# A mixture of experts whose scatters add into one table, with the combining spread over three engines

## The chip, the cores and the metric

One core of a Trainium2 chip runs the whole program. The metric is the device time of one execution in microseconds, as the median of several runs. The engines are TensorE (PE, with its weight loads as PEld), VectorE (DVE), ScalarE (ACT), GpSimd (POOL) and SyncE (SP). SP and POOL issue the data transfers (DMAs) that matter here: SP the plain ones, POOL the indirect ones, in which each of 128 partitions names its own row in memory.

## What is computed

The input is 8 sequences of 1024 tokens, 128 features each, in float32. A Mamba-style mixer and an MLP come first, and then the mixture of experts, in which the change lies. Cut to that part:

```python
x = x + _layernorm(_L0_attn_ref(_layernorm(x), ...))
x = x + _layernorm(_L0_ffn_ref(_layernorm(x), ...))

# _L0_ffn_ref, E = 8 experts, K = 2 of them for each token, N = 8192 tokens
probs = softmax(x @ Wr + br)
gates, ids = top_k(probs, K)
cap = ceil(1.2 * N / E)                       # the best gated tokens of an expert, by rank
xg = x[disp_tok].reshape(E, cap, 128)         # gather of the tokens of each expert
h = silu(einsum(xg, W1) + b1)
out = einsum(h, W2) + b2
gated = out * disp_g
y = zeros((N, 128)).at[disp_tok].add(gated)   # a token gets the sum of up to two experts
```

## The kernel before, in words

The program is a chain of stages with a barrier between two of them: a first stage (normalisation and decays, to about 60 us), the scan (to about 349 us), the MLP with the routing logits (to 513 us), the choice of the tokens of each expert (to 613 us), the experts (to 832 us) and the combining (to the end). Within a stage each engine runs its own instruction stream in a written order, and semaphores (`need`, `wait_ge`) make it wait for the others.

**MLP.** 32 groups of two token tiles run through a software pipeline, `skewed8`, that names for each engine its steps and by how many groups each lags. The last two steps on TensorE are `turn_xl` (L1380, lag 11), which transposes the normalised group into the PSUM bank `pX`, and `route` (L1387, lag 12), which makes the logits in `pL`. Between them ScalarE copies `pX` to `xlT` (L1253); VectorE takes the logits (L1330). TensorE's order within a step is `route` of group g-1, then `turn_xl` of group g, and `turn_xl` waits until ScalarE has copied the group before out of the single bank.

**Experts.** The slots of the eight experts are 80 columns of 128 rows, in 24 blocks of 2 to 4 columns, three blocks for each expert. POOL's stream is `fetch` of block i (one gather of 128 token rows for each column, L1871) and then `leave` of block i-5 (one scatter of 128 result rows for each column, L1879). `leave` waits for the block's result `yo`, which VectorE multiplies by the gates (L1992) from the PSUM bank `e_pB` that TensorE filled. A token has two rows in the table `choice_rows`: one for its first expert and one for its other, at a distance of 8192 rows, and `choice_of` holds the row to which a slot writes. No row is written twice. SP zeroes the table in the first stage with 16 transfers (L259), since a dropped token leaves a row unwritten, and POOL waits for that before its first gather. In the experts' stage SP loads the weights, and then waits for the scatters of the last eight blocks (L1851).

**Combining.** 64 token tiles are 14 groups of four tiles and five narrow ones of 2, 2, 2, 1 and 1. For each group SP loads both rows of the tokens (L1854, L1855), TensorE adds them in PSUM by two products with the identity (L1931), VectorE takes statistics of each tile (L2000) and joins them (L2006), ScalarE takes the root (L1959), VectorE inverts it (L2012) and forms the shift (L2014), ScalarE normalises each tile out of PSUM (L1965), VectorE adds the residual `x1` (L2019), and SP stores the group (L1859). VectorE's order in a step is: statistics of group g, inverse and shift of g-1, joining of g, residual of g-2. SP keeps eight groups of loads ahead of its stores. Ahead of this TensorE runs 18 products on zeros (L1925).

Of the kernel before, what the change touches and what calls it, by code (L numbers as in the profile page):

```python
# [32 lines left out]
P = 128  # L33
# [20 lines left out]
FILLS = 2 * TOKENS // (8 * P)  # L54
ROWLEN = D + 2
STEEP = 2.0 ** 100
# [21 lines left out]
def skewed(eng, steps, unroll, head, stages):  # L78


    def at(i, which):
# [12 lines left out]
    for i in range(steps, steps + max(lag for lag, _ in stages)):  # L94
        at(i, None)


def build(nc, x, ln_w, ln_b, in_proj_w, conv_w, conv_b, dt_bias, A_log, D_skip, rms_w, out_proj_w,
          mlp_w1, mlp_b1, mlp_w2, mlp_b2, Wr, br, W1, b1, W2, b2, out):
    table = nc.dram_tensor("token_rows", (TOKENS, ROWLEN), F32, kind="Internal").ap()  # L100
    choice = nc.dram_tensor("choice_rows", (2 * TOKENS, D), F32, kind="Internal").ap()
    decays = nc.dram_tensor("decay_rows", (2, P, TILES * HEADS), F32, kind="Internal").ap()
    with ExitStack() as ctx:
# [49 lines left out]
        token_of, choice_of = (sb(n, [P, COLS], U32) for n in ("token_of", "choice_of"))  # L153
# [23 lines left out]
        with ExitStack() as st:  # L177
# [58 lines left out]
            def _(sp):  # L236
# [19 lines left out]
                zeros = choice.rearrange("(n p r) d -> n p (r d)", p=P, r=8)  # L256
# [881 lines left out]
        with ExitStack() as st:  # L1138
# [23 lines left out]
            pT, pX, pM0, pM1, pL = (pst("m_" + n) for n in ("pT", "pX", "pM0", "pM1", "pL"))  # L1162
# [16 lines left out]
            def skewed8(eng, stages):  # L1179

                skewed(eng, GROUPS, 8, 16, stages)
# [33 lines left out]
            def _(a):  # L1215
# [34 lines left out]
                def turned_xl(g, m):  # L1250
                    need(a, s_px, g)
                    need(a, s_pl, g, NB)
                    a.activation(xlT[:, m % NB, :], pX[:, 0:N], ACT.Copy).then_inc(s_xlT, 1)  # L1253
# [92 lines left out]
            def _(pe):  # L1346
# [42 lines left out]
                skewed8(pe, [(5, down), (3, up), (12, route), (2, turn), (11, turn_xl)])  # L1389


        with ExitStack() as st:
# [186 lines left out]
            def _(v):  # L1579
# [156 lines left out]
                link(v.scalar_tensor_tensor(out=acc[:, 1, :], in0=is_other[:, :], scalar=float(TOKENS - TILES), in1=vacant[:, :],  # L1736
                                            op0=ALU.mult, op1=ALU.add))
                link(v.tensor_copy(choice_of[:, :], acc[:, 1, :]))
# [6 lines left out]
        with ExitStack() as st:  # L1745
# [16 lines left out]
            def pst(name, shape=[P, 512]):  # L1762
# [12 lines left out]
            widths = [CG] * 14 + [2, 2, 2, 1, 1]  # L1775
# [4 lines left out]
            yb = arena2[:, 0:TILES * D].rearrange("p (t d) -> p t d", d=D)  # L1780
# [6 lines left out]
            (s_ys2, s_st, s_var, s_sd, s_rs, s_sh, s_yna, s_ot, s_out) = (  # L1787
                sem("c_" + n) for n in ("ys", "st", "var", "sd", "rs", "shift", "yna", "ot", "out"))
            first_v = choice[0:TOKENS].rearrange("(p s b) d -> s p b d", s=STEPS, p=P)
            other_v = choice[TOKENS:2 * TOKENS].rearrange("(p s b) d -> s p b d", s=STEPS, p=P)  # L1790
            out_v = out.rearrange("b (s p) d -> s p b d", p=P)

            def of_group(g):
                return slice(first_tile[g], first_tile[g + 1])

# [13 lines left out]
            banks = pT + pH + [pO, pB]  # L1809
            BANKS = len(banks)  # L1810

            def summed(g):
                return banks[g % BANKS][:, 0:D * widths[g]]
# [27 lines left out]
            def _(sp):  # L1841
# [11 lines left out]
                def load(g):  # L1853
                    sp.dma_start(ys[:, of_group(g)], part(first_v, g)).then_inc(s_in[g], 16)  # L1854
                    sp.dma_start(yb[:, of_group(g)], part(other_v, g)).then_inc(s_in[g], 16)  # L1855

                def store(g):
                    need(sp, s_ot, g)
                    sp.dma_start(part(out_v, g), ys[:, of_group(g)]).then_inc(s_out, 16)  # L1859
# [4 lines left out]
            def _(g):  # L1864
# [10 lines left out]
                def leave(n):  # L1875
                    need(g, s_yo, n)
                    for i in range(sizes[n]):
                        c = starts[n] + i
                        g.indirect_dma_start(choice, bass.IndirectOffsetOnAxis(ap=choice_of[:, c:c + 1], axis=0),  # L1879
                                             yo[:, n % RING, i, :], None, bounds_check=2 * TOKENS - 1,  # L1880
                                             oob_is_err=False).then_inc(s_scat[n % RING], 16)
                g.wait_ge(filled, 16 * FILLS)
                staged([(0, fetch), (LAG, leave)])

            @block.tensor
            def _(pe):
# [40 lines left out]
                def both(g):  # L1927
                    pe.wait_ge(s_in[g], 32)
                    need(pe, s_yna, g, BANKS)
                    for f, first in ((ys, True), (yb, False)):  # L1930
                        ins = pe.matmul(summed(g), ident[:, :], f[:, of_group(g)].rearrange("p t d -> p (t d)"), start=first, stop=not first)  # L1931
                    ins.then_inc(s_ys2, 1)
                in_turn(GROUPS, [(0, both)])

            @block.scalar
            def _(a):
# [33 lines left out]
            def _(v):  # L1970
# [25 lines left out]
                def moments(g):  # L1996
                    need(v, s_var, g, 2)
                    need(v, s_ys2, g)
                    for i in range(widths[g]):
                        ins = v.bn_stats(c_st[:, g % 2, i, :], summed(g)[:, D * i:D * (i + 1)])  # L2000
# [16 lines left out]
                def add_x1(g):  # L2017
# [27 lines left out]
```

## Time and profile before

| what | us |
|---|---|
| median of 3 runs | 878.65 (876.77 to 880.98) |
| the profiled execution, whole time | 879.82 |
| its span, first to last instruction | 878.1 |
| experts' stage, first gather to first load of the combining | 613.64 to 832.75 |
| combining, first load to the end of the span | 832.75 to 878.1 |

The profile is of one execution, with times from the start of its span. A row of the timeline is: start in us, duration in us, engine, line of the program, operation, what it writes and reads, how many instructions the row merges, and in brackets how long the engine had been idle and what ended that. "issue" means that the engine waited for nothing that the profile shows. Shapes are partitions x elements. The whole time is 1.72 us more than the span, and the profiled execution is 1.17 us above the median.

### The profile page before, as it was taken

The numbers are of one execution on the slowest core, as the hardware profiler recorded it, in microseconds if no ns is written. First come the engines' busy times: TensorE is split into PE (matmuls) and PEld (weight loads), VectorE is DVE, ScalarE is ACT, GpSimd is POOL, SyncE is SP. The second block draws the span as 40 slices with busy tenths as digits, with TensorE's granted clock in tenths as the row PEclk, the third lists the DMA queues.
The fourth block names the chain that finished last, engine by engine and source line by source line (L and its number), as shares of the span: only waits on it lengthen the run. The fifth ranks groups of instructions, "written<-read, shape, count | busy, mean of one in ns | idle before, by whom it ended". The sixth has DMA issues, their size and how long they took to land. (4 is left out here: it accounts for less than half of the span.)

```text
span 878.1 us, 14619 instructions
## 1 busy us (share of the span) xinstructions
PE 710.7 (81%) x3872; PEld 493.1 (56%) x3872; DVE 606.9 (69%) x2161; ACT 490.8 (56%) x1207; POOL 442.8 (50%) x576
## 2 busy tenths in 40 slices
PE   7657999999999997899999721046698888888994
PEld 3425677777777775798989720023354444444442
DVE  7957999999999993799999868897111211121067
ACT  4864666676667675687877415434243432334157
POOL 7612767667667664234433350000757777777500
PEclk8867999999999999999999855555699998999998
DMA  9930000000000001500000004000322212221196
GB/s 219 388 129 14 1 1 1 2 1 1 2 1 1 1 1 34 159 1 2 3 1 1 1 0 196 0 0 2 99 64 72 74 50 74 73 75 50 41 352 219
DMA packets 50414, 52.92 MB, mean 60 GB/s; under 512 B 7576, under 2 KB 39624, under 8 KB 50080
## 3 DMA queue, kind: packets, MB, share of 16 engines
q1 hardware_dynamic: 44496, 41.62, 14.6%
q0 software_dynamic: 5120, 10.37, 4.4%
q8 instruction: 30, 0.49, 0.2%
q14 instruction: 48, 0.39, 0.1%
q10 hardware_dynamic: 720, 0.05, 0.1%
HBM read 28.04 MB, written 24.18 MB: 59 GB/s over the span
## 5 line engine op out<-in xcount | busy, mean ns | idle before, releaser
L890 DVE SCALAR_TENSOR_TENSOR s_cv<-s_pU,tap_w,s_cv 128x256 f32<-128x256 f32 x372 | 153.4, 476 | 12.4 <-ACT s_cv L821 12.0
L1871 POOL DMA_INDIRECT arena<-token_rows,token_of x80 | 81.4, 1017 | 112.3 <-issue 111.7
L1992 DVE TENSOR_TENSOR arena<-e_pB,e_gate 128x384 f32<-128x384 f32 (+2 forms) x24 | 14.5, 603 | 123.9 <-PE e_pB L1916 123.9
L1879 POOL DMA_INDIRECT choice_rows<-arena,choice_of x80 | 79.7, 996 | 32.7 <-issue 22.6
L1943 ACT ACTIVATE e_h<-e_pH,e_bcols 128x384 f32<-128x384 f32 (+2 forms) x96 | 58.7, 616 | 65.6 <-PE e_pH L1900 63.1
L1900 PE MATMUL e_pH<-e_xgT,e_w 128*128 128x384 f32 (+2 forms) x192 | 83.4, 584 | 0.0
L689 POOL TENSOR_TENSOR s_xa<-s_xt,arena 128x512 f32<-128x512 f32 x32 | 34.5, 1077 | 88.3 <-ACT s_xt L839 88.3
L821 ACT ACTIVATE s_cv<-s_pU,tap_b,tap_w 128x256 f32<-128x256 f32 x124 | 63.7, 561 | 23.4 <-PE s_pU L723 23.0
L723 PE MATMUL s_pU<-arena,w_in 128*128 128x262 f32 x248 | 69.3, 403 | 7.7 <-DVE s_cv L890 3.4
L1908 PE MATMUL e_pO<-e_h,e_w 128*128 128x384 f32 (+2 forms) x192 | 72.7, 522 | 0.4 <-ACT e_oT L1950 0.4
L1372 PE MATMUL m_pM<-w_m,m_h 128*128 128x128 f32 x512 | 62.5, 275 | 0.1
L1363 PE MATMUL m_pH<-m_hT,w_m 128*128 128x256 f32 x256 | 60.7, 380 | 2.1 <-ACT m_h L1246 1.5
L1372 PEld LDWEIGHTS m_pM<-w_m,m_h 128*128 128x128 f32 x512 | 59.7, 192 | 0.3 <-issue 0.3
L1900 PEld LDWEIGHTS e_pH<-e_xgT,e_w 128*128 128x128 f32 x192 | 40.1, 220 | 28.9 <-issue 21.2
L1908 PEld LDWEIGHTS e_pO<-e_h,e_w 128*128 128x128 f32 x192 | 36.7, 191 | 33.3 <-issue 20.6
L1207 POOL TENSOR_TENSOR arena<-arena,m_un 128x256 f32<-128x256 f32 (+1 forms) x32 | 22.5, 703 | 64.9 <-DVE m_un L1282 64.9
L723 PEld LDWEIGHTS s_pU<-arena,w_in 128*128 128x128 f32 x248 | 43.0, 197 | 17.0 <-DVE s_cv L890 7.6
L1363 PEld LDWEIGHTS m_pH<-m_hT,w_m 128*128 128x128 f32 x256 | 46.2, 190 | 7.5 <-ACT m_hT L1239 2.6
L1246 ACT ACTIVATE m_h<-m_pH,b_col 128x256 f32<-128x256 f32 x128 | 50.2, 485 | 0.0
L1984 DVE COPY e_xgT<-e_pT 128x384 f32<-128x384 f32 (+2 forms) x24 | 14.4, 599 | 48.3 <-PE e_pT L1891 48.3
L1950 ACT ACTIVATE e_oT<-e_pO,e_bcols 128x384 f32<-128x384 f32 (+2 forms) x24 | 14.8, 617 | 54.8 <-PE e_pO L1908 54.8
L701 POOL TENSOR_TENSOR s_y<-s_y,s_dx 128x512 f32<-128x512 f32 x32 | 40.9, 1277 | 4.9 <-DVE s_y L923 4.9
(305 smaller groups left out, 1874.3 us busy)
## 6 DMA issues: line engine op xcount, KB each, us to landing
choice_rows<-zrow SPq DMA_DIRECT2D x16, 512.0 KB, 7.7
arena<-choice_rows SPq DMA_DIRECT2D x28, 256.0 KB, 5.3
token_rows<-arena SPq DMA_DIRECT2D x8, 520.0 KB, 5.8
n_x<-in_L_attn_x_dram SPq DMA_DIRECT2D x8, 512.0 KB, 7.6
arena<-in_L_attn_x_dram SPq DMA_DIRECT2D x8, 512.0 KB, 4.8
e_w<-in_L_ffn_W_dram SPq DMA_DIRECT2D x16, 256.0 KB, 3.2
out_dram<-arena SPq DMA_DIRECT2D x14, 256.0 KB, 4.2
decay_rows<-arena SPq DMA_DIRECT2D x2, 1024.0 KB, 4.8
```

Source lines behind the costliest of these rows:

```text
L701: g.tensor_tensor(y2[:, :], y1[:, p % 2, :], dx[:, p % 4, :], ALU.add).then_inc(s_y2, 1)
L723: pe.matmul(pU[m % 2][:, 0:G2 * XBLK], w_in[:, P * m:P * (m + 1)], xT[:, G2 * p:G2 * (p + 1), :].rearrange("p t c -> p (t c)"), start=True ...
L821: a.activation(by_tile(cv[:, p % 2, m, :]), columns(m)[:, :, 0:P], ACT.Identity, bias=tap_b[:, m:m + 1], scale=tap_w[:, m, 0:1]).then_inc( ...
L890: v.scalar_tensor_tensor(out=by_tile(cv[:, p % 2, m, :]), in0=columns(m)[:, :, tap:tap + P], scalar=tap_w[:, m, tap:tap + 1], in1=by_tile( ...
L1246: ins = a.activation(h1[:, m % NB, c, :], pH[half_][:, N * (c % 2):N * (c % 2 + 1)], ACT.Relu, bias=b1_col[:, c:c + 1])
L1363: ins = pe.matmul(pH[half_][:, N * c:N * (c + 1)], w_m1[:, P * f:P * (f + 1)], hT[:, m % NB, :], start=True, stop=True)
L1372: ins = pe.matmul(pM[m % 2][:, P * i:P * (i + 1)], h1[:, m % NB, c, P * i:P * (i + 1)], w_m2[:, c, :], start=(c == 0), stop=(c == NF - 1))
L1871: g.indirect_dma_start(xg[:, n % RING, i, :], None, table, bass.IndirectOffsetOnAxis(ap=token_of[:, c:c + 1], axis=0), bounds_check=TOKENS ...
L1879: g.indirect_dma_start(choice, bass.IndirectOffsetOnAxis(ap=choice_of[:, c:c + 1], axis=0), yo[:, n % RING, i, :], None, bounds_check=2 * ...
L1900: pe.matmul(pH[c][:, 0:w], we1[:, expert(n) % 2, P * c:P * (c + 1)], xgT[:, n % 3, 0:w], start=True, stop=True).then_inc(s_ph, 1)
L1908: ins = pe.matmul(pO[:, 0:w], we2[:, expert(n) % 2, c, :], hb[:, n % 2, c, 0:w], start=(c == 0), stop=(c == NF - 1))
L1943: a.activation(hb[:, n % 2, c, 0:w], pH[c][:, 0:w], ACT.Silu, bias=bcols[:, f:f + 1]).then_inc(s_h, 1)
```

## The change

Five things are changed.

1. The table `choice_rows` of 16384 rows becomes `summed_rows` of 8192, one row for each token; both experts of a token scatter into the same row, and the scatter adds to what is there (`compute_op=ALU.add`). `target_of` takes the place of `choice_of`. SP zeroes it with 8 transfers.
2. A token's two experts are never the same, so no two scatters of one expert meet in a row, but those of two experts can. Ahead of an expert's first block POOL therefore waits until all scatters of the expert before have landed.
3. In the combining SP loads one row for each token, and TensorE has no part in it; statistics and normalisation read SBUF. In the 14 wide groups ScalarE normalises three tiles, VectorE the fourth (`normal_last`), and GpSimd adds the residual (`add_x1_wide`). In the five narrow groups ScalarE normalises and VectorE adds, as before. The 18 products on zeros are gone.
4. In the MLP `pX` becomes two banks, and in the last steps, when no new group enters, TensorE runs `turn_xl` of group g ahead of `route` of group g-1 (`at_end`).
5. The threshold `STEEP`, from which a slower way through the scan is chosen, goes from 2^100 to 2^62.

The core of the diff:

```diff
-FILLS = 2 * TOKENS // (8 * P)
+FILLS = TOKENS // (8 * P)
-STEEP = 2.0 ** 100
+STEEP = 2.0 ** 62
...
     for i in range(steps, steps + max(lag for lag, _ in stages)):
-        at(i, None)
+        at(i, None, at_end or stages)
...
-                for n in range(2 * TOKENS // (8 * P)):
+                for n in range(FILLS):
                     sp.dma_start(zeros[n], zrow[:, :]).then_inc(filled, 16)
...
+            pX = [pst("m_pX0"), pst("m_pX1")]
...
-                    need(pe, s_xlT, g, 1)
+                    need(pe, s_xlT, g, 2)
                     for i in range(G):
-                        ins = pe.transpose(pX[:, P * i:P * (i + 1)], xl[:, m % NB, i, :], ident[:, :])
+                        ins = pe.transpose(pX[m % 2][:, P * i:P * (i + 1)], xl[:, m % NB, i, :], ident[:, :])
...
-                skewed8(pe, [(5, down), (3, up), (12, route), (2, turn), (11, turn_xl)])
+                skewed8(pe, [(5, down), (3, up), (12, route), (2, turn), (11, turn_xl)],
+                        at_end=[(5, down), (3, up), (11, turn_xl), (12, route), (2, turn)])
...
                 def load(g):
-                    sp.dma_start(ys[:, of_group(g)], part(first_v, g)).then_inc(s_in[g], 16)
-                    sp.dma_start(yb[:, of_group(g)], part(other_v, g)).then_inc(s_in[g], 16)
+                    sp.dma_start(ys[:, of_group(g)], part(summed_v, g)).then_inc(s_in[g], 16)
...
                 def leave(n):
                     need(g, s_yo, n)
+                    if expert(n) and n % STEP == 0:
+                        for m in range(n - STEP, n):
+                            g.wait_ge(s_scat[m % RING], 16 * blocks_upto(m))
                     for i in range(sizes[n]):
                         c = starts[n] + i
-                        g.indirect_dma_start(choice, bass.IndirectOffsetOnAxis(ap=choice_of[:, c:c + 1], axis=0),
-                                             yo[:, n % RING, i, :], None, bounds_check=2 * TOKENS - 1,
-                                             oob_is_err=False).then_inc(s_scat[n % RING], 16)
+                        g.indirect_dma_start(summed, bass.IndirectOffsetOnAxis(ap=target_of[:, c:c + 1], axis=0),
+                                             yo[:, n % RING, i, :], None, bounds_check=TOKENS - 1, oob_is_err=False,
+                                             compute_op=ALU.add).then_inc(s_scat[n % RING], 16)
...
+                def add_x1_wide(g_):
+                    need(g, s_yna, g_)
+                    need(g, s_ynv, g_)
+                    g.tensor_tensor(yn[:, of_group(g_)], yn[:, of_group(g_)], x1[:, of_group(g_), :], ALU.add).then_inc(s_otp, 1)
+                in_turn(WIDE_GROUPS, [(0, add_x1_wide)])
...
-                need(pe, s_xgT, TOTAL - 1)
-                for _ in range(18):
-                    pe.matmul(pT[0][:, :], ones[:, :], zrow[:, 0:512], start=True, stop=True)
...
-                    for i in range(widths[g]):
+                    for i in range(on_act(g)):
                         t = first_tile[g] + i
-                        ins = a.activation(ys[:, t, :], summed(g)[:, D * i:D * (i + 1)], ACT.Identity, bias=c_sh[:, g, i:i + 1], scale=c_rs[:, g, i:i + 1])
+                        ins = a.activation(yn[:, t, :], ys[:, t, :], ACT.Identity, bias=c_sh[:, g, i:i + 1], scale=c_rs[:, g, i:i + 1])
...
-                        ins = v.bn_stats(c_st[:, g % 2, i, :], summed(g)[:, D * i:D * (i + 1)])
+                        ins = v.bn_stats(c_st[:, g % 2, i, :], ys[:, first_tile[g] + i, :])
...
+                def normal_last(g):
+                    if g < WIDE_GROUPS:
+                        t = first_tile[g] + CG - 1
+                        need(v, s_rs, g)
+                        v.tensor_scalar(yn[:, t, :], ys[:, t, :], c_mv[:, g, CG - 1, 0:1], c_rs[:, g, CG - 1:CG],
+                                        ALU.subtract, ALU.mult).then_inc(s_ynv, 1)
...
-                in_turn(GROUPS, [(0, moments), (1, inverse), (0, combined), (2, add_x1)])
+                in_turn(GROUPS, [(0, moments), (1, inverse), (0, combined), (1, normal_last), (2, add_x1_narrow)])
```

On POOL, near the end of the experts' stage, before: the last two gathers (of block 23) stand between the scatters of blocks 17 and 18; then only scatters follow. `e_yo` is VectorE's result; the names at the gathers are the semaphores that say a ring buffer is free.

```order
L1879 DMA choice_rows<-arena,choice_of 16384x128 x2
L1871 DMA arena<-token_rows,token_of 128x130 [waits s_row,n_shifted,s_mr]
L1871 DMA arena<-token_rows,token_of 128x130
L1879 DMA choice_rows<-arena,choice_of 16384x128 [waits e_yo]
L1879 DMA choice_rows<-arena,choice_of 16384x128 x3
```

The same place now; block 18 is the first of expert 6. `n_post`, `n_pre` and `n_convs` are earlier names of the semaphores that count the scatters of blocks 15 to 17.

```order
L1884 DMA summed_rows<-arena,target_of 8192x128 x2
L1873 DMA arena<-token_rows,token_of 128x130 [waits s_xfirst,s_row,s_mm]
L1873 DMA arena<-token_rows,token_of 128x130
L1884 DMA summed_rows<-arena,target_of 8192x128 [waits n_post,n_pre,n_convs,e_yo]
L1884 DMA summed_rows<-arena,target_of 8192x128 x3
```

The order of gathers and scatters is the same; seven scatters (the first of experts 1 to 7) now also wait for three blocks' landings. Ahead of that of expert 7, block 21, stand no gathers, only the scatters of blocks 19 and 20. The fourteen residual adds stand behind the last scatter on this engine.

On VectorE, one step of the combining in its steady part, before:

```order
L2000 BN_STATS c_stats<-e_pH 128x6 x4
L2012 RECIPROCAL c_rs<-c_sd 128x4
L2014 SCALAR_TENSOR_TENSOR c_shift<-c_mv,c_rs 128x4
L2006 BN_AGGR c_mv<-c_stats 128x2 x4
L2019 TENSOR_TENSOR arena<-arena 128x512
```

and now:

```order
L1999 BN_STATS c_stats<-arena 128x6 x4
L2011 RECIPROCAL c_rs<-c_sd 128x4
L2013 SCALAR_TENSOR_TENSOR c_shift<-c_mv,c_rs 128x4
L2005 BN_AGGR c_mv<-c_stats 128x2 x4
L2020 TENSOR_SCALAR arena<-arena,c_mv,c_rs 128x128
```

The statistics read SBUF (`arena`) in place of PSUM, and the residual add over four tiles has become the normalisation of one.

## Rows read from the trace of the kernel before

**Rows 1.** Windows: us; PE, PEld, DVE, ACT, POOL busy (count); PEclk; DMA share; GB/s.

```profile
613.00:832.00 219.00, 183.12 (x570) 101.46 (x571) 35.63 (x120) 76.25 (x123) 161.02 (x160) 0.91 0.25 67
832.00:878.10 46.10, 33.80 (x88) 15.62 (x86) 32.48 (x185) 27.83 (x83) 0.00 (x0) 0.92 0.83 275
```

**Rows 2.** The page's costliest groups: the gathers and the scatters.

```profile
L1871 POOL DMA_INDIRECT arena<-token_rows,token_of x80 | 81.4, 1017 | 112.3 <-issue 111.7
L1879 POOL DMA_INDIRECT choice_rows<-arena,choice_of x80 | 79.7, 996 | 32.7 <-issue 22.6
```

**Rows 3.** Timeline of POOL and SP, experts' stage to the combining's first load.

```profile
613.64 1.26 POOL L1871 DMA_INDIRECT arena<-token_rows,token_of  x1 [88.18 <-issue]
...
798.56 0.98 POOL L1879 DMA_INDIRECT choice_rows<-arena,choice_of  x1 [0.30 <-issue]
...
802.52 1.02 POOL L1879 DMA_INDIRECT choice_rows<-arena,choice_of  x1 [0.30 <-issue]
...
815.74 0.98 POOL L1879 DMA_INDIRECT choice_rows<-arena,choice_of  x1 [0.30 <-issue]
818.90 0.98 POOL L1879 DMA_INDIRECT choice_rows<-arena,choice_of  x1 [2.18 <-DVE arena L1992]
...
830.49 0.98 POOL L1879 DMA_INDIRECT choice_rows<-arena,choice_of  x1 [0.30 <-issue]
832.75 0.33 SPq L1854 DMA_DIRECT2D arena<-choice_rows  x1
```

**Rows 4.** DMA issues: what, queue, count, KB each, us from issue to landing.

```profile
arena<-token_rows,token_of POOLq DMA_INDIRECT x80, 2.6
choice_rows<-arena,choice_of POOLq DMA_INDIRECT x80, 2.3
e_w<-in_L_ffn_W_dram SPq DMA_DIRECT2D x16, 256.0 KB, 3.2
```

**Rows 5.** Timeline of VectorE in the combining: first, one steady step, last.

```profile
838.73 0.89 DVE L2000 BATCH_NORM_STATS2 c_stats<-e_pT 128x6 f32<-128x128 f32 x4 [16.75 <-PE e_pT L1931]
...
845.46 0.88 DVE L2000 BATCH_NORM_STATS2 c_stats<-e_pH 128x6 f32<-128x128 f32 x4
846.46 0.16 DVE L2014 SCALAR_TENSOR_TENSOR c_shift<-c_mv,c_rs 128x4 f32<-128x4 f32 x1
846.83 0.66 DVE L2019 TENSOR_TENSOR arena<-arena 128x512 f32<-128x512 f32 x1
847.40 0.88 DVE L2000 BATCH_NORM_STATS2 c_stats<-e_pH 128x6 f32<-128x128 f32 x4
...
874.43 0.29 DVE L2019 TENSOR_TENSOR arena<-arena 128x128 f32<-128x128 f32 x1 [0.24 <-ACT arena L1965]
```

**Rows 6.** Timeline, first stage: VectorE's shift beside a GpSimd operation.

```profile
22.66 1.47 POOL L307 TENSOR_TENSOR n_hn<-n_hc,n_scale 128x768 f32<-128x768 f32 x1
23.08 1.08 DVE L525 SCALAR_TENSOR_TENSOR n_shift<-moments,n_scale 128x8 f32<-128x8 f32 x1
```

**Rows 7.** All of line L525: count, ns min/median/max, first and last start.

```profile
L525 DVE SCALAR_TENSOR_TENSOR n_shift<-moments,n_scale x8: 1076/1080/1372, 10.2 to 32.0; 128x8 f32<-128x8 f32 x8
```

**Rows 8.** Timeline, end of the MLP: normalisations on VectorE beside a GpSimd add.

```profile
486.39 0.59 DVE L1282 TENSOR_SCALAR m_un<-m_at,m_mv,m_rs 128x128 f32<-128x128 f32 x2
486.88 0.97 DVE L1282 TENSOR_SCALAR m_xl<-arena,m_mv,m_rs 128x128 f32<-128x128 f32 x2
487.05 0.72 POOL L1207 TENSOR_TENSOR arena<-arena,m_un 128x256 f32<-128x256 f32 x1 [1.84 <-DVE m_un L1282]
```

**Rows 9.** A page group: GpSimd's add of 128x512 in the scan.

```profile
L701 POOL TENSOR_TENSOR s_y<-s_y,s_dx 128x512 f32<-128x512 f32 x32 | 40.9, 1277 | 4.9 <-DVE s_y L923 4.9
```

**Rows 10.** Timeline of TensorE in the last groups of the MLP.

```profile
508.00 1.02 PE L1387 MATMUL m_pL<-w_r,m_xlT 128*128 128x8 f32 x4 [0.47 <-ACT m_xlT L1253]
508.88 0.67 PE L1380 MATMUL m_pX<-ident,m_xl 128*128 128x128 f32 x2
510.02 1.02 PE L1387 MATMUL m_pL<-w_r,m_xlT 128*128 128x8 f32 x4 [0.47 <-ACT m_xlT L1253]
```

More of the change, by code:

```diff
@@ L75, in need_apart, with skewed, at @@
         eng.sem_inc(carrier[0], 1)
-def skewed(eng, steps, unroll, head, stages):
-    def at(i, which):
+def skewed(eng, steps, unroll, head, stages, at_end=None):
+    def at(i, which, stages=stages):
         for lag, stage in stages:
@@ L151, in build @@
         ssq = sb("ssq", [P, TILES])
-        token_of, choice_of = (sb(n, [P, COLS], U32) for n in ("token_of", "choice_of"))
+        token_of, target_of = (sb(n, [P, COLS], U32) for n in ("token_of", "target_of"))
         is_other, is_first = (sb(n, [P, COLS]) for n in ("is_other", "is_first"))
@@ L1161, in build @@
             xlT = sbt("m_xlT", [P, NB, N])
-            pT, pX, pM0, pM1, pL = (pst("m_" + n) for n in ("pT", "pX", "pM0", "pM1", "pL"))
+            pT, pM0, pM1, pL = (pst("m_" + n) for n in ("pT", "pM0", "pM1", "pL"))
+            pX = [pst("m_pX0"), pst("m_pX1")]
             pM = [pM0, pM1]
@@ L1177, in build, with skewed8 @@
             block = st.enter_context(nc.Block())
-            def skewed8(eng, stages):
-                skewed(eng, GROUPS, 8, 16, stages)
+            def skewed8(eng, stages, at_end=None):
+                skewed(eng, GROUPS, 8, 16, stages, at_end)
             @block.sync
@@ L1735, in _ @@
                 link(v.tensor_tensor(vacant[:, :], vals[:, :], vacant[:, :], ALU.add))
[L1736 removed]
+                link(v.scalar_tensor_tensor(out=acc[:, 1, :], in0=is_other[:, :], scalar=-float(TILES), in1=vacant[:, :],
                                             op0=ALU.mult, op1=ALU.add))
[L1738 removed]
+                link(v.tensor_copy(target_of[:, :], acc[:, 1, :]))
                 link(v.scalar_tensor_tensor(out=vals[:, :], in0=is_other[:, :], scalar=-float(TILES), in1=vals[:, :],
@@ L1786, in build @@
             s_in = [sem(f"c_in{g}") for g in range(GROUPS)]
[L1787 to L1790, printed above, removed]
+            (s_st, s_var, s_sd, s_rs, s_sh, s_yna, s_ynv, s_otp, s_otv, s_out) = (
+                sem("c_" + n) for n in ("st", "var", "sd", "rs", "shift", "yna", "ynv", "otp", "otv", "out"))
+            summed_v = summed.rearrange("(p s b) d -> s p b d", s=STEPS, p=P)
             out_v = out.rearrange("b (s p) d -> s p b d", p=P)
@@ L1794, in of_group, with on_act @@
                 return slice(first_tile[g], first_tile[g + 1])
+            def on_act(g):
+                return CG - 1 if g < WIDE_GROUPS else widths[g]
             def part(v_, g):
@@ L1853, in load @@
                 def load(g):
-                    sp.dma_start(ys[:, of_group(g)], part(first_v, g)).then_inc(s_in[g], 16)
-                    sp.dma_start(yb[:, of_group(g)], part(other_v, g)).then_inc(s_in[g], 16)
+                    sp.dma_start(ys[:, of_group(g)], part(summed_v, g)).then_inc(s_in[g], 16)
                 def store(g):
-                    need(sp, s_ot, g)
-                    sp.dma_start(part(out_v, g), ys[:, of_group(g)]).then_inc(s_out, 16)
+                    if g < WIDE_GROUPS:
+                        need(sp, s_otp, g)
+                    else:
+                        need(sp, s_otv, g - WIDE_GROUPS)
+                    sp.dma_start(part(out_v, g), yn[:, of_group(g)]).then_inc(s_out, 16)
                 in_turn(GROUPS, [(0, load), (8, store)])
@@ L1921, in _ @@
                 staged([(2, up), (3, down), (4, back), (0, turn)])
-                need(pe, s_xgT, TOTAL - 1)
-                for _ in range(18):
-                    pe.matmul(pT[0][:, :], ones[:, :], zrow[:, 0:512], start=True, stop=True)
[L1927 to L1933, printed above, removed]
             @block.scalar
@@ L1997, in moments @@
                     need(v, s_var, g, 2)
-                    need(v, s_ys2, g)
+                    v.wait_ge(s_in[g], 16)
                     for i in range(widths[g]):
-                        ins = v.bn_stats(c_st[:, g % 2, i, :], summed(g)[:, D * i:D * (i + 1)])
+                        ins = v.bn_stats(c_st[:, g % 2, i, :], ys[:, first_tile[g] + i, :])
                     ins.then_inc(s_st, 1)
```

23 lines of the change are left out of this document (11 added, 12 removed).

## The prediction, made before the changed kernel ran

> **What bounds the kernel now.** I read the windows of the two changed stages first, then the costliest groups, then the timeline of POOL in the one and of VectorE in the other.
>
> In the experts' stage POOL is the bound. From the first gather at 613.64 to the last scatter at 830.49 it issues 160 indirect DMAs [rows 3]; a gather takes 1.017 us and a scatter 0.996 [rows 2], with 0.30 us behind each, and three steps of the stream, from the scatter at 798.56 to that at 802.52, take 3.96 us, so 1.32 each [rows 3]. 160 of these are 211 us of the 217 between those rows. TensorE is busy for 183 of the stage's 219 us [rows 1], but POOL issues a block's gathers five blocks ahead of its scatters, so what TensorE does is late only at the end, where the POOL rows show waits for VectorE's results (2.18 us before 818.90).
>
> In the combining VectorE is the bound. Its step for a wide group is 1.94 us (statistics at 845.46, the next at 847.40) and has no gap: 1.00 to the shift at 846.46, 0.37 to the residual add at 846.83, 0.57 to the next statistics [rows 5]. It starts late, 5.98 us after the first load (832.75 to 838.73), since a group needs two loads and TensorE's sum first [rows 3, 5].
>
> In the last groups of the MLP nothing is busy throughout. One group follows another at 2.02 us (508.00 to 510.02) on a ring: route, then the transposition 0.88 later, then 1.14 until ScalarE's copy lets the next route start [rows 10].
>
> **Edit 4, the MLP's end.** With two banks the transposition of group g runs ahead of the route of g-1, and the copy runs beside that route. What is left on TensorE is 0.88 for the route and 0.67 for the transposition [rows 10], 1.55 a group in place of 2.02. Four groups at the end go at this pace, so 4 x 0.47 = -1.9 us. The bounds are 0 (if VectorE's inputs are late instead) and six groups, -2.8. In the loop the order is unchanged and its wait was met by the route before it, so nothing moves there.
>
> **Edits 1 and 5, the tables and the threshold.** The eight zero-fills that go stand on SP's queue behind the loads that the first stage waits for, and POOL asks for them only before 613.64: nothing. The threshold matters only if the inputs cross it; from the reference's own inputs the largest exponent of the decays within half a chunk is about 2^35, under both thresholds, so the same way is taken.
>
> **Edit 1, the scatter that adds.** Their count and place on POOL stay. No row shows an adding scatter. The nearest rows are gather and scatter, which move rows in opposite directions and differ by 0.02 us [rows 2]: I take no extra time on POOL. The bound from above is an adding scatter as dear as one gather and one scatter together, since it reads the row and writes it: 80 x 1.02 = +82 us. A gain has no reason, as nothing is left out of the instruction.
>
> The Trainium skill (DMA: Bandwidth & Descriptors, "Anatomy of one DMA") says that generating descriptors is a small part of a DMA from GpSimd, and that many can be emitted before it shows. By it the extra time is near zero, as taken; no row here varies the number.
>
> Landing is the second cost. A plain scatter lands 2.3 us after its issue, a gather 2.6 [rows 4]. An adding one lies between 2.3 and a gather and a scatter in turn, 4.9; I take +1.0, nearer to the plain one, because the row in memory can be read while the row in SBUF is.
>
> **Edit 2, the waits.** Ahead of the first block of an expert, POOL now waits for the last scatter of the expert before. Between the two stand the gathers of a later block. At expert 6 there are two: the scatter at 798.56, the next at 802.52, so 3.96 us of cover against a landing of 3.3 [rows 3, 4]. Experts 1 to 5 have three or four gathers, 5.3 us or more. Both cover it, and cost nothing; without that cover each would cost a landing. Behind the waiting scatter on POOL stand the gathers for later blocks, five blocks ahead of need. At expert 7 no gather is left: the scatter at 818.90 follows that at 815.74 and already waits there for VectorE [rows 3], so of the landing the extra 1.0 is exposed. The same 1.0 is exposed behind the last scatter (830.49), for which SP waits before the first load (832.75). Together +2.0 us, between 0 and 5.2.
>
> **Edit 3, the combining.** It starts earlier: one load of 256 KB, which lands in 3.2 us where little else runs [rows 4], and no sum on TensorE. VectorE starts 3.3 us after the first load in place of 5.98.
>
> VectorE's own step becomes 1.00 + 0.37 as now, and 0.25 for one tile's normalisation (two stand at 486.39 and the next at 486.88 [rows 8]) where the add took 0.57: 1.62 us. ScalarE has three tiles in place of four. But GpSimd now adds 128x512 for each group, and that took 1.277 us [rows 9]. The rows show what VectorE does beside such an operation. A shift of 128x8 takes 1.08 us, all eight of them [rows 6, 7], and ends when GpSimd's does (22.66 + 1.47 = 24.13; 23.08 + 1.08 = 24.16); the same operation over 128x4 takes 0.16 where GpSimd is idle [rows 5]. Two tiles normalised take 0.59 us alone and 0.97 beside GpSimd's add [rows 8]. These are the very two operations, shift and normalisation, that stand in VectorE's new step. So shift, joining and normalisation (0.08 + 0.29 + 0.25 = 0.62 us) and the 1.277 of GpSimd exclude each other but for the joining. At best GpSimd starts behind the normalisation, and a step is 1.28 + 0.62 + 0.1 for two hand-overs = 2.0 us. At worst it starts between shift and normalisation, and a step is 1.62 + 1.28 less the joining, 2.6. I take 2.3, the middle, since GpSimd's start hangs on ScalarE and falls in either place. That is more than the 1.94 of now.
>
> The sum from the first load: 3.3 to start, 1.2 and 1.6 for two steps before GpSimd has work, 12 x 2.3 = 27.6, together 33.7. The narrow groups took from 866.8 (845.46 + 11 x 1.94) to the end of VectorE at 874.72 (874.43 + 0.29), 7.9 us [rows 5]; two wide adds of 0.57 leave this stretch and one normalisation enters, 7.0. Together 40.7 against 42.0 now (832.75 to 874.72): -1.3 us. With 2.0 a step it is -4.9, with 2.6 +2.3. The store behind is the same, and the loads, half as many, run ahead.
>
> **The sum.** -1.9 (MLP) + 2.0 (landings) - 1.3 (combining) = -1.2. On the profiled 879.82 that is 878.6; this execution lies 1.17 above the median, so the forecast for the median is 877.5 us. A measurement of this kernel can tell about 0.5%, 4.4 us, from no change.
>
> **Rivals.** *VectorE is not held up.* If GpSimd's adds fall so that VectorE's two operations miss them, or the exclusion doesn't hold here, the step is 1.62: 3.3 + 1.2 + 1.6 + 12 x 1.62 + 7.0 = 32.5, 9.5 us less than now, and the kernel takes 869. For it speaks that only two short operations of each step are at risk; against it the eight of eight shifts [rows 7].
>
> *POOL pays for the adding.* If the adding makes POOL write three ends of a transfer for a row (source, old value, result) where a plain one has two, and its time goes by what it writes, each scatter takes half of 0.996 more [rows 2]: 80 x 0.5 = +40, so 917. It decides from 0.07 us a scatter on, which makes 80 x 0.07 = 5.6 against the -1.2. For it speaks that POOL has no slack in this stage [rows 1 to 3]; against it that POOL's two kinds cost the same.
>
> The Trainium skill (Collectives: The Full Stack, "Why ReduceScatter is half of AllGather") says that a transfer that reduces emits two reading descriptors for each chunk where a copy emits one. No row here shows whether POOL's time follows it; by it this rival's 917 would be the time.
>
> *The landings are not covered.* If an adding scatter lands after 8 us, five boundaries stall for 2.7 and one for 4.0, and expert 7 and the end each show 5.7: 29 us, so 904 with the other terms. It decides from a landing of 5.5 us on. Against it speak 2.3 and 2.6 [rows 4].
>
> **How the numbers follow.** The forecast has 0.40, with its own range of 871 to 882: MLP 0 to -2.8, landings 0 to 5.2, steps of 2.0 to 2.6. Of it 0.10 falls below 874 (steps near 2.0), 0.28 within 0.5%, 0.02 above. VectorE not held up has 0.30, POOL's price 0.22, uncovered landings 0.08. So faster 0.40, same 0.28, slower 0.32. The range goes from 867, under the first rival with a little more at the MLP's end, to 900, which takes in an extra 0.28 us a scatter; what is left out is the upper part of the other two rivals, some 0.15, and little below.
>
> **What would show it.** Right: scatters of 1.0 us with 1.3 from start to start; POOL's first scatters of experts 1 to 6 without a wait, that of expert 7 about 1 us later; shift and normalisation in the wide groups often near 1 us in place of 0.16 and 0.33, a step of about 2.3 us; last logits about 2 us sooner. Wrong: scatters longer than 1.07 us; waits at the boundaries; a VectorE step of 1.6.

## The result: the adding is paid on POOL

The changed kernel takes 919.6 us (median of 4 runs, 919.4 to 920.68) against 878.36 for the kernel before (876.77 to 880.98): a ratio of 1.0467, 95% interval 1.0451 to 1.0483. It is slower by 41 us, outside the range given. The profiled execution took 919.78, with a span of 917.7.

The costliest groups of the changed kernel (line, engine, operation, count; busy us and mean ns of one; idle time ahead of it), its software queue that carries gathers and scatters (packets, MB, share), and the scatter's landing:

```profile
L1873 POOL DMA_INDIRECT arena<-token_rows,token_of x80 | 82.5, 1031 | 112.3 <-issue 110.2
L1884 POOL DMA_INDIRECT summed_rows<-arena,target_of x80 | 126.2, 1578 | 29.7 <-issue 23.2
...
q0 software_dynamic: 14080, 10.37, 8.6%
...
summed_rows<-arena,target_of POOLq DMA_INDIRECT x80, 3.3
```

Against [rows 2] the gather has kept its price and the scatter has gone from 996 to 1578 ns. In the kernel before the same queue line reads:

```profile
q0 software_dynamic: 5120, 10.37, 4.4%
```

The bytes are the same and the packets are not. 5120 packets over 160 transfers are 32 each; 14080 less 80 gathers of 32 leave 144 for a scatter, 128 rows and 16 more. Landing is 3.3 us where it was 2.3 [rows 4].

POOL and SP at the places of [rows 3], in the timeline of the changed kernel (start, duration, engine, line; in brackets the idle time and what ended it):

```profile
610.83 1.26 POOL L1873 DMA_INDIRECT arena<-token_rows,token_of  x1 [88.22 <-issue]
...
849.12 1.55 POOL L1884 DMA_INDIRECT summed_rows<-arena,target_of  x1 [0.30 <-issue]
850.98 1.55 POOL L1884 DMA_INDIRECT summed_rows<-arena,target_of  x1 [0.30 <-issue]
854.96 1.55 POOL L1884 DMA_INDIRECT summed_rows<-arena,target_of  x1 [2.42 <-DMA summed_rows<-arena,target_of]
...
871.72 1.56 POOL L1884 DMA_INDIRECT summed_rows<-arena,target_of  x1 [0.31 <-issue]
874.90 4.23 SPq L1854 DMA_DIRECT2D arena<-summed_rows  x9
```

From start to start a scatter now takes 1.86 us (849.12 to 850.98); the 0.30 between two is as before. The stage from first gather to last scatter is 260.89 us, where it was 216.85. The only place where POOL waits for the landing of earlier scatters is the row at 854.96, the first scatter of expert 7. Its windows, columns as in [rows 1], for the experts and the combining:

```profile
610.00:874.00 264.00, 182.07 (x545) 101.01 (x545) 35.94 (x120) 76.12 (x123) 208.66 (x160) 0.84 0.35 56
874.00:917.70 43.70, 0.00 (x0) 0.00 (x0) 34.91 (x185) 24.75 (x69) 18.13 (x14) 0.50 0.64 193
```

POOL's busy time in the experts' stage goes from 161.02 to 208.66 with the same 160 instructions; TensorE's stays at 182, so it is further from the bound than before.

Where the spans differ, stretch by stretch, in us:

| stretch | before | after | difference |
|---|---|---|---|
| to the first gather | 613.64 | 610.83 | -2.8 |
| first gather to last scatter | 216.85 | 260.89 | +44.0 |
| last scatter to first load | 2.26 | 3.18 | +0.9 |
| first load to first statistics | 5.98 | 2.52 | -3.5 |
| first statistics to VectorE's end | 35.99 | 36.15 | +0.2 |
| VectorE's end to the end of the span | 3.38 | 4.13 | +0.8 |
| sum | 878.10 | 917.70 | +39.6 |

### The profile page after: what moved, and what is told of

Same layout as the page of the kernel before. It is cut to its first block and busy times, and to the rows that moved or that the text cites. A ratio compares the mean times of both kernels' runs of the same rounds, so it can differ in the third digit from the quotient of the medians.

```text
span 917.7 us, 14384 instructions
## 1 busy us (share of the span) xinstructions
PE 672.7 (73%) x3760; PEld 475.2 (52%) x3760; DVE 609.7 (66%) x2161; ACT 487.5 (53%) x1193; POOL 508.6 (55%) x590
## 3 DMA queue, kind: packets, MB, share of 16 engines
q0 software_dynamic: 14080, 10.37, 8.6%
## 5 line engine op out<-in xcount | busy, mean ns | idle before, releaser
L1884 POOL DMA_INDIRECT summed_rows<-arena,target_of x80 | 126.2, 1578 | 29.7 <-issue 23.2
L1911 PE MATMUL e_pH<-e_xgT,e_w 128*128 128x384 f32 (+2 forms) x192 | 91.5, 631 | 0.0
L1911 PEld LDWEIGHTS e_pH<-e_xgT,e_w 128*128 128x128 f32 x192 | 44.3, 243 | 33.6 <-issue 29.1
L1902 PE MATMUL e_pT<-ident,arena 128*128 128x128 f32 x80 | 17.3, 342 | 58.0 <-DMA arena<-token_rows,token_of 58.0
L1204 POOL TENSOR_TENSOR m_h0b<-m_h,b2row 128x256 f32<-128x256 f32 x32 | 23.3, 730 | 38.1 <-DVE m_h L1303 38.1
```

The lines of the kernel that those rows point to most:

```text
L1884: g.indirect_dma_start(summed, bass.IndirectOffsetOnAxis(ap=target_of[:, c:c + 1], axis=0), yo[:, n % RING, i, :], None, bounds_check=TOKE ...
L1911: pe.matmul(pH[c][:, 0:w], we1[:, expert(n) % 2, P * c:P * (c + 1)], xgT[:, n % 3, 0:w], start=True, stop=True).then_inc(s_ph, 1)
```

## The experiments

**The adding taken away.** If the adding alone costs, the changed kernel without it must fall back under the kernel before; if the shared table or the waits cost, it must not.

```diff
-                                             yo[:, n % RING, i, :], None, bounds_check=TOKENS - 1, oob_is_err=False,
-                                             compute_op=ALU.add).then_inc(s_scat[n % RING], 16)
+                                             yo[:, n % RING, i, :], None, bounds_check=TOKENS - 1, oob_is_err=False).then_inc(s_scat[n % RING], 16)
```

> The changed kernel with one thing undone: its scatters overwrite in place of adding (the addition in the scatter is left out, so a token's row holds one expert's result alone). One table, waits between experts, the new combining and the MLP's end stay. Theory: the adding alone makes a scatter dearer on POOL (1.58 us in place of 1.00), and nothing else lengthens the experts' stage. Then scatters take 1.00 us, 1.30 from start to start, the stage takes 217 us in place of 260.9, the landing falls from 3.3 to 2.3 us, and the whole time is 919.6 - 44 - 1 = about 874.5, under the kernel before. Rival: the one table of half the rows, or the waits between experts, make the scatters slow (rows in one table written by neighbouring experts, a queue that is drained seven times). Then scatters stay near 1.6 us and the time near 919.

It takes 875.95 us, 0.9973 of the kernel before (0.9956 to 0.9991). The scatter's group, and the first scatter of expert 7 in the timeline:

```profile
L1884 POOL DMA_INDIRECT summed_rows<-arena,target_of x80 | 79.6, 995 | 31.0 <-issue 22.9
...
813.81 0.98 POOL L1884 DMA_INDIRECT summed_rows<-arena,target_of  x1 [2.18 <-DVE arena L1990]
```

The scatter is back at 995 ns with one table and all seven waits in place, and the stage is 214.83 us. Of the 2.0 us by which this is under the kernel before, 1.6 are a shorter wait for VectorE ahead of the first scatter (3.52 us in place of 5.16), which the kernel with the MLP's end alone has too (3.50), with its scatters as they were. The wait for expert 6's landings is met while POOL waits for VectorE as before. So with plain scatters neither the shared table nor the waits cost anything; the adding does.

**The adding alone, in the kernel before.**

```diff
-                                             oob_is_err=False).then_inc(s_scat[n % RING], 16)
+                                             oob_is_err=False, compute_op=ALU.add).then_inc(s_scat[n % RING], 16)
```

> The kernel before with one thing added: its scatters add to the zeroed two-row table, where no row is written twice. No waits between experts, no other combining, no change in the MLP. Theory (the adding is the price): scatters take 1.57 us, 1.86 from start to start, 80 x 0.57 = 45.6 us more, of which the 2 us that POOL waited for VectorE near the end come back, and 0.9 more for the last landing: 878.4 + 45.6 - 2 + 0.9 = 923. Rival (waits or the shared table are the price): scatters stay at 1.0 us, and the time within 3 us of 878.

It takes 924.23 us, a ratio of 1.0523 (1.0492 to 1.0554). Its scatters, their landing, and the first scatter of expert 7:

```profile
L1879 POOL DMA_INDIRECT choice_rows<-arena,choice_of x80 | 126.2, 1578 | 27.7 <-issue 22.9
...
choice_rows<-arena,choice_of POOLq DMA_INDIRECT x80, 3.3
...
859.00 1.55 POOL L1879 DMA_INDIRECT choice_rows<-arena,choice_of  x1 [0.30 <-DVE arena L1992]
```

The price is the changed kernel's to the nanosecond, with no row written twice and no wait. With a slower POOL, VectorE is no longer late at 859.00 (2.18 us before). The stage is 258.79 us, 2.1 less than the changed kernel's 260.89: the 2.42 of the one exposed landing less the 0.30 that stands behind every scatter.

**What the price hangs on.** Two kernels with a different shape of scatter for each expert, one adding, one not:

```diff
+            SHAPES = [(P, D), (96, D), (64, D), (32, D), (16, D), (P, D // 2), (P, D // 4), (P, D)]
...
+                        r, w = SHAPES[expert(n)]
+                        to = summed if w == D else summed.rearrange("t (h d) -> (t h) d", d=w)
+                        g.indirect_dma_start(to, bass.IndirectOffsetOnAxis(ap=target_of[0:r, c:c + 1], axis=0),
+                                             yo[0:r, n % RING, i, 0:w], None, bounds_check=TOKENS - 1,
```

> The changed kernel with a different shape of scatter for each expert, all of them adding: expert 0 128 rows of 512 B, expert 1 96 rows, expert 2 64, expert 3 32, expert 4 16 rows of 512 B, expert 5 128 rows of 256 B, expert 6 128 rows of 128 B, expert 7 128 rows of 512 B (the remaining rows and columns of the results are left out, and the short rows go to other places of the table). To be read against the same shapes without the adding. Theory (POOL writes more for each row): the extra goes with the rows and not with the bytes: 0.58 us for 128 rows, 0.43 for 96, 0.29 for 64, 0.14 for 32, 0.07 for 16, and 0.58 again for 256 B and 128 B, in 128 + 16 packets a scatter. Rival 1 (a fixed cost of the adding kind): 0.58 in all of them. Rival 2 (bytes, or an adding transfer that moves slower and holds POOL back): 0.29 for 64 rows and for 256 B, 0.15 for 32 rows and for 128 B; the first scatters, which find an empty queue, would be shorter than the rest.

> The same eight shapes without the adding (it is left out, with the rows and columns named for the adding one). It gives the plain price for each shape. Theory: 1.00 us for 128 rows whatever their bytes, and less for fewer rows if POOL's time has a part for each row; if the plain time were all for rows, 0.5 for 64. Rival (a fixed cost): 1.00 for all rows.

The two kernels take 911.80 and 872.55 us, one run each; what is read is the single scatters. The last scatter of expert 0 (128 rows of 512 B), 2 (64 rows), 4 (16 rows) and 6 (128 rows of 128 B) in the timeline, and the queue's packets; first adding, then plain:

```profile
667.42 1.55 POOL L1888 DMA_INDIRECT summed_rows<-arena,target_of  x1 [0.30 <-issue]
729.18 1.41 POOL L1888 DMA_INDIRECT summed_rows<-arena,target_of  x1 [0.30 <-issue]
788.65 1.29 POOL L1888 DMA_INDIRECT summed_rows<-arena,target_of  x1 [0.30 <-issue]
843.38 1.55 POOL L1888 DMA_INDIRECT summed_rows<-arena,target_of  x1 [0.30 <-issue]
...
q0 software_dynamic: 11040, 8.12, 7.3%
```

```profile
663.82 0.98 POOL L1888 DMA_INDIRECT summed_rows<-arena,target_of  x1 [0.30 <-issue]
714.79 0.90 POOL L1888 DMA_INDIRECT summed_rows<-arena,target_of  x1 [0.30 <-issue]
764.71 0.84 POOL L1888 DMA_INDIRECT summed_rows<-arena,target_of  x1 [0.30 <-issue]
810.69 0.98 POOL L1888 DMA_INDIRECT summed_rows<-arena,target_of  x1 [0.30 <-issue]
...
q0 software_dynamic: 5120, 8.12, 3.9%
```

The last scatter of each expert, in us:

| shape | adding | plain | extra |
|---|---|---|---|
| 128 rows of 512 B | 1.55 | 0.98 | 0.57 |
| 96 rows | 1.42 | 0.92 | 0.50 |
| 64 rows | 1.41 | 0.90 | 0.51 |
| 32 rows | 1.32 | 0.86 | 0.46 |
| 16 rows | 1.29 | 0.84 | 0.45 |
| 128 rows of 256 B | 1.55 | 0.98 | 0.57 |
| 128 rows of 128 B | 1.55 | 0.98 | 0.57 |

The theory falls: with an eighth of the rows the extra is still 0.45 us where 0.07 was expected. The rival with the bytes falls too: rows of 128 B cost what rows of 512 B cost, and the first adding scatter, with no other in the queue, takes 1.63 us (at 641.00) and is no shorter than the rest. Most of the extra, some 0.44 us by these rows, is there for any adding scatter, and only about 0.12 goes with the rows from 16 to 128, about 1 ns a row. It is nearest to the rival of a fixed cost; what POOL does in that fixed time no run here shows. The packets do follow the rows: ten scatters of each shape with rows + 16 packets (four times 144, then 112, 80, 48 and 32) and 80 gathers of 32 make the 11040; plain ones have 32 in every shape. So the packets are no measure of POOL's time: 144 packets in place of 32, for 128 rows in place of 16, came with 0.12 us more of the extra.

**The MLP's end alone.** The kernel before with edit 4 (`pX` in two banks, `at_end`) and nothing else.

```diff
-                skewed8(pe, [(5, down), (3, up), (12, route), (2, turn), (11, turn_xl)])
+                skewed8(pe, [(5, down), (3, up), (12, route), (2, turn), (11, turn_xl)],
+                        at_end=[(5, down), (3, up), (11, turn_xl), (12, route), (2, turn)])
```

> The kernel before with the change to the MLP's end alone: two banks for the transposition, and in the last steps the transposition ahead of the route. Theory: a group at the end takes 1.35 us in place of 2.02, as the trace of the changed kernel shows, in four steps or a little more, so the last logits come 1.8 to 2.8 us sooner and the whole time is 875.6 to 876.6. The changed kernel's MLP also began 1.05 us sooner than that of the kernel before; if this comes of the eight zero-fills that are gone, it isn't here, and the MLP begins near 349.4; if it is a difference from one execution to the next, it may be anywhere between 348.3 and 349.4. Rival: the MLP's gain is lost again behind it, since the choice of the tokens waits for something else; then the time stays at 878.4.

It takes 875.79 us, 0.9971 of the kernel before (0.9955 to 0.9986): shorter by 0.3%, clear of the noise but far under 2%, and the least time here of a version that computes everything. TensorE in the last groups, where [rows 10] showed 2.02 us a group:

```profile
505.92 0.69 PE L1381 MATMUL m_pX<-ident,m_xl 128*128 128x128 f32 x2
506.40 0.87 PE L1388 MATMUL m_pL<-w_r,m_xlT 128*128 128x8 f32 x4
507.13 0.67 PE L1381 MATMUL m_pX<-ident,m_xl 128*128 128x128 f32 x2
507.64 0.99 PE L1388 MATMUL m_pL<-w_r,m_xlT 128*128 128x8 f32 x4
508.49 0.67 PE L1381 MATMUL m_pX<-ident,m_xl 128*128 128x128 f32 x2
508.99 0.99 PE L1388 MATMUL m_pL<-w_r,m_xlT 128*128 128x8 f32 x4
510.34 0.99 PE L1388 MATMUL m_pL<-w_r,m_xlT 128*128 128x8 f32 x4 [0.36 <-DVE logits L1331]
```

A route follows the last at 1.24 to 1.35 us, without a gap on TensorE until the last. In the changed kernel the MLP also begins 1.05 us sooner than in the kernel before (348.31 against 349.36), and so it does here. The first row of the MLP on VectorE tells that the zero-fills and the threshold are not the cause, since this kernel has all sixteen fills and the old threshold. First this kernel, then the kernel before:

```profile
348.22 0.61 DVE L1303 SCALAR_TENSOR_TENSOR m_h<-arena,m_rooty,m_res 128x128 f32<-128x128 f32 x2
```

```profile
349.36 0.35 DVE L1302 SCALAR_TENSOR_TENSOR m_h<-arena,m_rooty,m_res 128x128 f32<-128x128 f32 x1
```

In the kernel with the adding alone, which lacks edit 4 too, it stands at 349.50. Nor does edit 4 bring the lead by itself: the kernel with the plain shapes has it and begins the MLP at 349.36, and over all nine profiles this row lies between 347.67 and 349.50. The lead's cause stays open. Little of it lasts in the changed kernel: at the fifth route from the end it leads by only 0.08 us (503.93 against 504.01).

**The combining's split, undone in two ways.** In the changed kernel, first ScalarE takes all tiles and VectorE all residual adds again; then GpSimd's add is left out and nothing put in its place.

```diff
             def on_act(g):
-                return CG - 1 if g < WIDE_GROUPS else widths[g]
+                return widths[g]
...
-                in_turn(WIDE_GROUPS, [(0, add_x1_wide)])
...
-                in_turn(GROUPS, [(0, moments), (1, inverse), (0, combined), (1, normal_last), (2, add_x1_narrow)])
+                in_turn(GROUPS, [(0, moments), (1, inverse), (0, combined), (2, add_x1_narrow)])
```

> The changed kernel with the combining's split undone alone: ScalarE normalises all tiles and VectorE adds the residual in all groups, as in the kernel before, and GpSimd has no part. One load for a group and statistics from SBUF stay. Theory (GpSimd's add and VectorE's short operations exclude each other, which made a step 2.12 us): without GpSimd a step is VectorE's 1.00 + 0.37 + 0.57 = 1.94 us or a little less, the shift stays near 0.16 us, and with 14 groups the time is 2 to 3 us less than the changed kernel's, 917. Rival (the step of 2.12 is ScalarE's or the loads'): the step stays at 2.1 or grows, since ScalarE has four tiles again, and the time is 919.6 or above.

```diff
-                        need(sp, s_otp, g)
+                        need(sp, s_yna, g)
+                        need(sp, s_ynv, g)
...
-                in_turn(WIDE_GROUPS, [(0, add_x1_wide)])
```

> The changed kernel with GpSimd's residual add left out (the wide groups lack the residual), so that VectorE's step stands alone with three tiles on ScalarE and one on VectorE. Theory (exclusion): shift back to 0.16 us, a tile's normalisation to 0.3 us in all groups, a step of 1.62 us, so 14 x 0.5 = 7 us less than the changed kernel in the combining, about 912. Rival (the step was the loads' or ScalarE's): the step stays near 2.1.

What these are to be compared with is the combining of the changed kernel, VectorE and POOL in one view of the timeline each, over three groups:

```profile
881.78 0.87 DVE L1999 BATCH_NORM_STATS2 c_stats<-arena 128x6 f32<-128x128 f32 x4
...
883.23 1.32 DVE L2020 TENSOR_SCALAR arena<-arena,c_mv,c_rs 128x128 f32<-128x128 f32 x1
884.47 0.86 DVE L1999 BATCH_NORM_STATS2 c_stats<-arena 128x6 f32<-128x128 f32 x4
...
885.44 0.70 DVE L2013 SCALAR_TENSOR_TENSOR c_shift<-c_mv,c_rs 128x4 f32<-128x4 f32 x1
...
886.36 0.31 DVE L2020 TENSOR_SCALAR arena<-arena,c_mv,c_rs 128x128 f32<-128x128 f32 x1
...
887.93 0.31 DVE L2020 TENSOR_SCALAR arena<-arena,c_mv,c_rs 128x128 f32<-128x128 f32 x1
888.16 0.86 DVE L1999 BATCH_NORM_STATS2 c_stats<-arena 128x6 f32<-128x128 f32 x4
```

```profile
883.21 1.26 POOL L1893 TENSOR_TENSOR arena<-arena 128x512 f32<-128x512 f32 x1 [0.21 <-ACT arena L1964]
884.87 1.26 POOL L1893 TENSOR_TENSOR arena<-arena 128x512 f32<-128x512 f32 x1 [0.40 <-ACT arena L1964]
888.00 1.37 POOL L1893 TENSOR_TENSOR arena<-arena 128x512 f32<-128x512 f32 x1 [1.87 <-ACT arena L1964]
```

GpSimd adds from 883.21 to 884.47. VectorE's normalisation, issued at 883.23, ends at 884.55 and takes 1.32 us; the shift at 885.44 ends at 886.14, with GpSimd's next add (884.87 + 1.26 = 886.13). With GpSimd idle the normalisation at 886.36 takes 0.31, and so does that at 887.93, which starts just ahead of GpSimd's third add; there the add is the longer one, 1.37 in place of 1.26. The statistics keep their 0.86 in either case. Three groups take 888.16 - 881.78 = 6.38 us, 2.13 each.

With GpSimd's add left out, one step reads:

```profile
886.60 0.86 DVE L1999 BATCH_NORM_STATS2 c_stats<-arena 128x6 f32<-128x128 f32 x4
...
887.57 0.16 DVE L2013 SCALAR_TENSOR_TENSOR c_shift<-c_mv,c_rs 128x4 f32<-128x4 f32 x1
...
887.94 0.31 DVE L2020 TENSOR_SCALAR arena<-arena,c_mv,c_rs 128x128 f32<-128x128 f32 x1
888.17 0.86 DVE L1999 BATCH_NORM_STATS2 c_stats<-arena 128x6 f32<-128x128 f32 x4
```

The step is 1.57 us, all 14 normalisations lie between 310 and 319 ns and all 19 shifts between 158 and 164, and the kernel takes 911.04 (one run). From the first load to VectorE's end it is 31.71 us (874.80 to 906.51) in place of 38.67 in the changed kernel (874.90 to 913.57). So GpSimd's add costs VectorE 7 us here, and the loads and ScalarE allow the shorter step.

With the adds on VectorE two steps take 3.93 us (the statistics at 885.63 and 889.56), 1.97 each, and the shifts are back at 0.16. First load to VectorE's end is 37.78 us (873.83 to 911.61), 0.9 less than with GpSimd: less than the 2 to 3 expected. Early in the stretch VectorE waits 0.55 for ScalarE, which normalises four tiles again. The whole time, 919.89 (916.59 to 921.08), can't be told from the changed kernel's 919.6. So the split over three engines brings nothing over the split over two.

## Why the prediction was wrong

**Edit 1, extra time on POOL: the step that failed.** I took the adding scatter's time from the gather and the plain scatter, because they agreed, and set the extra to nothing. Both rows are of transfers that only copy; that they agree says that the direction doesn't matter, and nothing on a third kind of work. The bounds for an operation that no row showed were 0 and 1.02 us a scatter, with nothing to place it near either; the middle, 0.5, would have given 917, and my range stopped at 0.28. The scatters measured 0.58 more, 126.2 - 79.7 = 46.5 us, on an engine with no slack in this stage, which [rows 1 to 3] had shown rightly. The stage's +44.0 is 45.9 of these, for the 79 scatters that lie between its two ends, plus 1.1 for gathers 14 ns longer, less 3.0 for POOL's other waits. Those waits are, first before and then after:

```profile
644.84 1.03 POOL L1879 DMA_INDIRECT choice_rows<-arena,choice_of  x1 [5.16 <-DVE arena L1992]
...
813.17 0.98 POOL L1879 DMA_INDIRECT choice_rows<-arena,choice_of  x1 [1.90 <-DVE arena L1992]
```

```profile
640.36 1.64 POOL L1884 DMA_INDIRECT summed_rows<-arena,target_of  x1 [3.47 <-DVE arena L1991]
```

The first is 1.7 shorter, the second falls from 1.90 to the usual 0.30, and at expert 7 a landing of 2.42 stands where VectorE took 2.18. The first is not the slower POOL's doing, since the kernel without the adding has 3.52 there; against that kernel the stage is longer by 46.1 (260.89 against 214.83). The prediction let POOL wait for VectorE only at the end of the stage; the row at 644.84 shows that it waits at its start as well.

**The rival "POOL pays for the adding"** gave 917 and came within 3 us. Its mechanism was only part right, so that the closeness is in part luck. It let the time go by what POOL writes for a row, half of 0.996; the size, 0.58, is near, but the shapes show that it is mostly no matter of rows. The Trainium skill (Collectives: The Full Stack, "Why ReduceScatter is half of AllGather") gives two reading descriptors for a chunk that is reduced where a copy has one; the sum it led to was right in size, and the runs here can't show the descriptors themselves. The Trainium skill (DMA: Bandwidth & Descriptors, "Anatomy of one DMA") calls descriptor generation small and says that many descriptors can be emitted before the cost shows. The trace agrees with the second part, since 112 rows more cost a plain scatter 0.14 us and an adding one 0.26. But issuing can't be left out of the sum here: POOL is busy with it for 208.66 of 264 us, and its time per transfer sets the stage.

**Landing** came out as taken, 3.3 us for 2.3 + 1.0; the 1.0 was a choice, and no run here shows the reason given for it. **The waits** were right for experts 1 to 6, where no scatter waits for a landing; at expert 7 and at the end the extra was 0.24 (2.42 against 2.18) and 0.92, together 1.2 where +2.0 was taken. For expert 7 the 1.0 doesn't follow from the prediction's own rows: a landing of 3.3 from 815.74 ends at 819.04, only 0.14 behind the 818.90 at which VectorE let POOL go. That the slower POOL would at the same time let VectorE catch up, so that all of the landing's wait is exposed, was not in the prediction.

**Edit 4** was right in mechanism and too small: 1.24 to 1.35 us a group in place of the 1.55 taken, since the transposition holds the route back by only 0.5 (505.92 to 506.40) and the next transposition follows a route by 0.73 to 0.85 (506.40 to 507.13, 507.64 to 508.49), where 0.67 and 0.88 were taken. Over the last four steps that is 8.02 to 5.27 us, -2.75 and not -1.9; some 0.2 is given back one group earlier, where the transposition waits for VectorE ahead of the route. The routes at the two ends, before and after:

```profile
504.01 0.99 PE L1387 MATMUL m_pL<-w_r,m_xlT 128*128 128x8 f32 x4 [0.70 <-DVE logits L1330]
...
512.03 1.02 PE L1387 MATMUL m_pL<-w_r,m_xlT 128*128 128x8 f32 x4 [0.47 <-ACT m_xlT L1253]
```

```profile
503.93 0.86 PE L1388 MATMUL m_pL<-w_r,m_xlT 128*128 128x8 f32 x4
...
509.20 0.99 PE L1388 MATMUL m_pL<-w_r,m_xlT 128*128 128x8 f32 x4 [0.36 <-DVE logits L1331]
```

**Edit 3** was right in mechanism. Shift and normalisation are held up until GpSimd ends, and the step, 2.13, lies between the 2.0 and 2.6 given. From the first load to VectorE's end the combining is 38.67 in place of 41.97 us, -3.3 where -1.3 was taken: 12 x 0.17 less for the step and 0.8 less for a start at 2.52 in place of 3.3, but 0.9 more in the narrow groups (905.70 to 913.57, 7.9 where 7.0 was taken), whose first two shifts take 0.94 and 0.63 us beside GpSimd's last adds. Two groups in three are held up, the third not, since GpSimd's third add waits for ScalarE and falls between VectorE's two operations. The rival "VectorE is not held up" gave 32.5 us for this stretch, and 31.71 is what came when GpSimd's add was left out; with it in place the condition of that rival held in one group of three.

**Edits 1 and 5, the fills and the threshold**: nothing seen of either. The 1.05 us by which the MLP begins sooner are not theirs, as the kernel with the MLP's end alone shows.

## What to carry to other kernels

An adding indirect transfer is another instruction than a copying one: until a row of it is at hand, price it between once and twice the copy, and where the issuing engine bounds the stage count that price for every instruction. Here the summing that the scatters took over cost 46.5 us on the bounding engine, while the combining, which lost the summing on TensorE and half of its loads, became 3.3 us shorter. Since most of the price is there for any number of rows, smaller adding scatters don't lower it in proportion, and splitting one into two halves would raise it: by the rows above two of 64 rows hold POOL for 2 x 1.41 us where one of 128 takes 1.55 (an estimate, not run).

## What the runs showed of the hardware

- An adding scatter holds POOL for 1.55 to 1.64 us, a plain one for 0.98 to 1.03 (128 rows of 512 B). The extra is about 0.44 us fixed and 1 ns a row, the same at 512, 256 and 128 B a row.
- It goes out in one packet a row and 16 more (144 for 128 rows), where a plain one has 32 whatever its rows; it lands in 3.3 us in place of 2.3.
- The plain scatter's own price is mostly fixed as well: 0.84 us for 16 rows, 0.98 for 128.
- Beside GpSimd's 128x512 add of 1.26 us, VectorE's shift took 0.70 us for 128x4 and up to 0.94 for 128x2 (0.16 alone) and its normalisation of 128x128 up to 1.32 (0.31 alone), both ending with it; where the normalisation started first, the add took 1.37. Statistics from SBUF kept their 0.86 for four tiles.
